# Counting edge rows in pairs: a graph network kernel whose adjacency counts run between the blocks of its first projection

## The reference

```python
norm_x = t5_layer_norm(hidden_states, ln_weight)        # rows scaled by 1/rms, then by a weight
out = norm_x @ W_root + bias                            # 1024 x 286
for r in range(2):                                      # two edge types
    w = (edge_type == r)
    sums = segment_sum((norm_x[src] @ W_rel[r]) * w[:, None], dst)
    cnt  = segment_sum(w, dst)
    out  = out + sums / maximum(cnt, 1.0)[:, None]
y = elu(out) @ wo_weight
```

## Time and profile before

| | |
|---|---|
| median of three runs | 577.02 us |
| the profiled execution: time | 575.35 us |
| the profiled execution: span | 573.5 us |
| instructions | 8850 |
| TensorE matmul busy, whole span | 556.0 us (97%) |
| TensorE weight loads busy | 399.0 us (70%) |
| VectorE busy | 371.2 us (65%) |
| ScalarE busy | 243.3 us (42%) |
| GpSimd busy | 101.6 us (18%) |
| mean granted TensorE clock | 0.994 |

### The profile page before, as it was taken

The page is one execution under the profiler, slowest core; times in us unless marked ns, Lnnn a source line. Parts: engine busy times, 40 slices in busy tenths (PEclk is TensorE's granted clock), DMA queues, the critical chain, the costliest instruction groups (busy, mean ns, idle before and its releaser), DMA issues.

```text
span 573.5 us, 8850 instructions
## 1 busy us (share of the span) xinstructions
PE 556.0 (97%) x2708; PEld 399.0 (70%) x2708; DVE 371.2 (65%) x1070; ACT 243.3 (42%) x484; POOL 101.6 (18%) x80
## 2 busy tenths in 40 slices
PE   7999999999999999999999999999999999999992
PEld 3555555555598989888889888868868867555541
DVE  8588888888748898987331130048658667855555
ACT  3553464636565555652222121023232233367555
POOL 4010000000000000030544442102202220132130
PEclk9999999999999999999999999999999999999997
DMA  8511000111031312147200001500100100022123
GB/s 263 159 38 36 24 25 24 36 36 36 2 93 38 73 37 72 37 136 210 101 2 0 0 0 40 191 1 1 38 0 0 37 0 2 0 73 68 39 73 107
DMA packets 20963, 30.77 MB, mean 54 GB/s; under 512 B 5458, under 2 KB 15404, under 8 KB 20928
## 3 DMA queue, kind: packets, MB, share of 16 engines
q1 hardware_dynamic: 20512, 29.66, 17.6%
q10 hardware_dynamic: 416, 0.67, 0.4%
HBM read 25.20 MB, written 5.12 MB: 53 GB/s over the span
## 4 chain that ended last, share of the span: by engine, by line
PE 77%; DVE 9%; DVEq 5%; issue 5%; DMA 2%; SPq 1%; ACT 1%; POOL 0%
PE banks L989 12%; PE banks L1075 12%; PE banks L906 12%; PE banks L781 7%; PE banks L874 5%; PE banks L1011 5%; PE banks L1001 4%; PE banks L937 4%; PE banks L939 4%; DVEq L1251 3%; PE banks L916 3%; PE banks L1065 3%; DVE cnt L1259 2%; DVE oh_both L1239 2%; DVE oh_both L1234 1%
## 5 line engine op out<-in xcount | busy, mean ns | idle before, releaser
L781 PE MATMUL banks<-w_all,xnT 128*125 128x429 f32 x320 | 131.8, 535 | 1.3 <-DMA w_all<-in_L_gnn_W_rel 1.3
L781 PEld LDWEIGHTS banks<-w_all,xnT 128*125 128x125 f32 x320 | 54.0, 188 | 30.4 <-issue 28.6
L906 PE MATMUL banks<-hT,w_s 128*128 128x250 f32 x320 | 68.9, 375 | 0.1
L906 PEld LDWEIGHTS banks<-hT,w_s 128*128 128x128 f32 x320 | 60.3, 190 | 8.4 <-issue 1.4
L937 PE MATMUL banks<-y_hi,adj 125*125 125x288 f32 x200 | 55.2, 304 | 0.5 <-issue 0.5
L1259 DVE TENSOR_TENSOR cnt<-cnt,banks 125x110 f32 x160 | 42.4, 265 | 18.1 <-issue 12.6
L939 PE MATMUL banks<-y_lo,adj 125*125 125x286 f32 x200 | 53.5, 295 | 0.0
L1406 DVE TENSOR_SCALAR hT<-banks,g_c,b_c 128x125 f32<-128x125 f32 x60 | 19.4, 399 | 45.1 <-PE banks L891 45.0
L989 PE MATMUL banks<-adj,h_hi 125*128 125x250 f32 (+1 forms) x180 | 48.3, 367 | 0.2
L759 PEld LDWEIGHTS banks<-oh_both,oh_low 125*128 125x128 bf16 x320 | 23.1, 98 | 34.9 <-issue 20.1
L989 PE MATMUL banks<-adj,h_lo 125*128 125x250 f32 (+1 forms) x180 | 45.7, 353 | 0.0
(11 more groups left out here) (222 smaller groups left out, 943.0 us busy)
## 6 DMA issues: line engine op xcount, KB each, us to landing
xt<-in_x SPq DMA_DIRECT2D x15, 448.0 KB
out_x<-ot SPq DMA_DIRECT2D x9, 448.0 KB
w_s<-in_L_gnn_W SPq DMA_DIRECT2D x5, 512.0 KB, 6.4
xn<-in_x SPq DMA_DIRECT2D x5, 448.0 KB
wd_s<-in_L_gnn_Wd SPq DMA_DIRECT2D x1, 2048.0 KB, 13.5
w_all<-in_L_gnn_W_rel SPq DMA_DIRECT2D x6, 286.0 KB, 6.7
wo_s<-in_L_gnn_wo_weight SPq DMA_DIRECT2D x1, 1024.0 KB, 6.1
w_all<-in_L_gnn_W_root SPq DMA_DIRECT2D x3, 286.0 KB, 6.3
```

The costliest lines, as they stand in the source:

```text
L781: ins = pe.matmul(pb[0:P, 2 + 2 * v + n, 0:FH], xnT[:, u], w_all[:, u, n * FH:(n + 1) * FH], start=(u == 0), stop=(u == KD - 1))
L906: ins = pe.matmul(pb[:, b0 if f == 0 else 4 + f % 2, 0:2 * P], w1_s[:, k, f * 128:(f + 1) * 128], hT[:, k], start=(k == 0), stop=(k == KD ...
```

## The change

TensorE's order in `tile_of_1` changes. A row is no longer counted ahead of each block. At even blocks two rows are counted directly behind each other, at odd blocks none; the ninth row of a tile is counted at the last block, and `turn(1, v)` and `turn(0, 1 - v)` stand behind the pair at blocks 0 and 4. The number of instructions that compute, their waits, the buffers and all other engines' lists stay as they were.

```diff
-                extra = rows - KD
                 for u in range(KD):
-                    row(u if u <= 4 else u + extra)
+                    if u % 2 == 0:
+                        row(u)
+                        row(u + 1)
+                    if u == KD - 1 and rows > KD:
+                        row(KD)
                     if u == 0:
                         pe.wait_ge(xnT_copied, 1 + t * 2)
                         turn(1, v)
...
                         if uses is not None:
                             pe.wait_ge(xs_in[1 - v], uses)
                             turn(0, 1 - v)
-                        if extra:
-                            row(5)
                     products(u, v)
```

## The result

| | before | with the change |
|---|---|---|
| median of four runs | 577.02 us (575.8 to 578.52) | 585.06 us (584.14 to 585.88) |
| ratio | | 1.0146 (95% interval 1.0126 to 1.0166) |
| span of the profiled execution | 573.5 us | 584.0 us |
| first count | 22.98 us | 25.52 us |
| first count to first aggregation product | 135.07 us | 143.01 us |

The account below looks back on a forecast made before the run. VectorE was taken as the bound by a hair; eight 15.69 us tile cycles, 2.31 us of loop-start waits and tile 9's end lengthened the stage by 7.2 us: 577.0 + 7.2 = 584.2 us, range 580.5 to 588.5.

Parts of the forecast that it names:

- VectorE is the bound by a hair: Kernel before: VectorE needs near 30 us per two tiles, TensorE alone 14.70 per tile; VectorE never stands idle.
- two T: T is four transposes on TensorE, 0.43 us each time; two are counted in TensorE's 14.70 us per tile.
- The cycle of 5.06 + 10.63 us: Row 6's count to next tile's row 1 through VectorE, 5.06; on to row 6 through TensorE, 10.63; tile 15.69.
- the sum: Forecast's addition of tile cycles, loop starts and tile 9's end: end at 164.58 against 157.42 us, 7.2 us more.
- C6: TensorE's count of a tile's row 6, 0.21 us; VectorE's place was to start 0.50 behind it.
- C1: TensorE's count of a tile's row 1; forecast to wait 1.22 us for row 1's one-hots.
- The loop tiles: Tiles 3, 5 and 7, beginning a VectorE loop pass: row 3 waits 0.77 us, tiles take 16.2 to 16.5.
- The price of the lock: VectorE's loss beside GpSimd's `y_lo` on the shared port: 0.82 us at loop starts, 0.57 in other tiles.
- The threshold that the prediction gave for a gain: The change gains only if a VectorE row takes under 1.15 us; the rows showed 1.56.
- Two counts directly behind each other: Paired counts on TensorE, not shown in the trace: extra cost taken as 0, bounded by 2.9 us in all.
- "Faster": Rival: TensorE is the bound, VectorE has room, 2.2 us of switches come off, 574.8 us; chance 0.05.
- "No change": Rival: VectorE is the only bound, so TensorE's order doesn't matter, 577 us; chance 0.06.

Follow-up runs that it names:

- `no_weighing_pairs`: The change with VectorE's weighing step left out, so both edge types are counted in one digit; 576.0 us.
- the spread order: Against the change, pairs only at blocks 0, 2, 4, rows 6 to 8 counted singly: 580.6 us; also without VectorE's weighing step, 572.4 us.

## Why the prediction was right

- *VectorE is the bound by a hair.* Shown from two sides: a shorter row, by leaving out a step or by writing out the loop, gives 14.70 us per tile, the sum of TensorE's own 8 blocks, 9 rows and two T.
- *The cycle of 5.06 + 10.63 us.* A plain tile was 15.69 by the sum and 15.72 to 15.74 in tiles 4, 6 and 8. C6 of tile 6 to C1 of tile 7 took 5.06 (116.94 to 122.00), and C1 waited 1.19 where 1.22 was summed. The dependence on VectorE's row was tested with rows of 1.56, 1.35 and 1.30 us, and on where rows 6 to 8 are counted. All followed the cycle to 0.3 us per tile, once the banks below are in it.
- *The loop tiles.* 16.46 by the sum, 16.38 measured; the wait at row 3 was 0.66 where 0.77 was summed. The price of the lock was read wrongly, though it cost little: the prediction took what VectorE's step beside `y_lo` grows by as what the row grows by. Before, the step grew by 0.82, but the row took 2.12 from place to place instead of 1.56, 0.56 more, mostly because the gap of 0.18 ahead of the next row fell under the long step. With the change, in tile 7, `y_lo` begins at 123.08 and VectorE's step at 123.17 takes 1.42 us instead of 0.42, 1.00 more; its row grew by 0.75 (122.68 to 124.99, 2.31 us). So the 0.82 of the sum was near the right size by luck: a longer step than it had, of which less reached the row.
- *What was under-sized.* To the end of tile 9, 7.2 us by the sum and 7.8 measured. Tiles 2 and 3 took 15.92 and 16.82, 0.6 us over the sum together. It stands in the kernel before too: there they took 14.92 and 15.74, against 14.84 and 15.27 for the tiles that the prediction read. In both kernels VectorE takes 1.84 and 2.42 us from row 8's first place in tiles 1 and 2 to the next tile's, and 1.59 and 2.12 in the later ones. The sum set an end made of ideal tiles against a measured end that held this, and so missed 0.6. What makes these two passages longer is not known. The last 0.1 of the stage's 7.9 is a longer gap ahead of the aggregation.
- *What was left out.* The two PSUM banks. Row 1 waits for row 8's second place as well as for its own one-hots. With a row of 1.56 the one-hots come last and the sum is right, but by 0.1 to 0.2 us only (C6 to C1 took 5.06, and 4.95 to 4.98 with the third one-hot buffer). The prediction had not worked this out; that the omitted wait changed nothing was luck. The threshold that the prediction gave for a gain, a row of 1.15 us, is not the only one: by the banks it is (3.84 - 0.59 - 1.08 - 0.15) / 2, some 1.0, an estimate from the times of `no_weighing_pairs`. At 1.30 it was the banks that held TensorE.
- *Two counts directly behind each other.* The open price was taken as 0 and is 0: 0.41 for the pair.
- *The rivals.* "Faster" needed room on VectorE; given that room, the three pairs of the spread order save 0.17 per tile. "No change", by the Trainium skill's rule of the busiest engine (Perfetto Trace Analysis, Identifying the Most-Contended Engine), named the right engine, but not what the edit did to it: an engine that is the bound loses whatever makes it wait, and an edit elsewhere can do that.

## What to carry to other kernels

When two engines hand work to each other through two buffers, the order on one is part of the other's pace. Taking both buffers at once leaves the maker idle until the pair is used, and then asks for both again; write down the cycle (which row, through which engine, back to which) and add it up before grouping. Where the maker is the bound, look first at what its loop costs it per item: here register work of 0.2 us per row, invisible in busy time, was worth more than any order of counts that was tried.

## What the runs showed that was not expected

The gap of 0.18 us "issue" per VectorE row was register work on the loop's counter ahead of the load of the offsets. Moving the load moved the gap, and a constant counter removed it though the load stayed. Writing out a loop of four passes took some 3 us off a kernel of 577. And the first count came anywhere between 22.9 and 26.0 us, at 25.52 and 23.98 with one kernel, mostly as TensorE's first two blocks took up to twice as long in some profiles, at the lower clock where the profile records it; that spread is over a third of the effect under study. The distance to the end of tile 9 inside the trace repeated to 0.03 us.
